# Four semaphores over the whole sequence of gathers, in place of one stop of GpSimd for every group

## The chip, the cores and the metric

One Trainium2 chip, one core. The metric is the device time of the kernel in microseconds (us); every time below is in us unless ns is written. TensorE is called PE, VectorE DVE, ScalarE ACT, GpSimd POOL and SyncE SP, as the profile does.

## The reference: what is computed

One layer of graph attention, and behind it a layer of six experts of which each node takes two. Cut to what matters:

```python
# x: (12500, 256); src, dst: (200000,), dst in rising order; dist: (200000, 1, 1); 4 heads of 64
ft = (layernorm(x) @ W).reshape(n, 4, 64)
e = e_src[src] + e_dst[dst];  e = where(e >= 0, e, 0.2 * e)
a = softmax of e over the edges with the same dst, times dist
x = x + segment_sum(ft[src] * a, dst)          # attention, the "main" stage
x = x + top-2-of-6 experts(layernorm(x))       # three matmul layers for each expert
```

`dst` is `12500 * u**2` for uniform `u`, sorted: the first blocks of nodes have very many edges, the last ones few.

## The kernel before

The kernel runs in stages. Early ones normalise `x`, multiply by `W` and store for every node a row of 264 float32 in DRAM (`table`: 256 features and 8 score words), bring the 200000 edges into columns, and write a plan (`plan`, from `sched`). Then comes `main_stage`, which the change touches, and then `experts`.

The edges are cut into `NG = 196` groups of `GE = 1024` edges, which is `GT = 8` tiles of 128. The nodes are cut into 98 blocks of 128. An *item* is one group together with one block in which it has edges; because both are in order there are 293 items: one for each group and one more for each block that begins. Early in the stage a group has hardly over one item, late it has two. An item does all eight tiles of its group, or four, when its block touches one half only. A *pair* is two finished blocks, whose sums are divided, added to `x`, normalised and stored; there are 49.

What each engine does in `main_stage`:

- POOL goes through the groups in order. For each it issues eight indirect DMAs (`gather(g)`, L1001), each of which fetches 128 rows of `table` (1056 bytes each) into the slot `g % RING` of `rows`; `RING = 4`. Before them it waits, from the fifth group on, that the slot is free (`slot_free`, L1007), and from the second on that the whole group before has landed (`gathered`, L1009). This second wait is the stop in question.
- SP waits that a group has landed and that its row of `dst` is spread (`announce`, L967 to L970), and then raises `group_ready`. In a loop over the groups it first waits, by the plan, that the last item of the group four back is multiplied (`weighted`, L988), raises `slot_free` (L989), issues the next spread of `dst` (`m_drow`, L961), and announces the group before.
- ACT makes for each item the one-hot by node (L1245 and L1248) once its group is announced, and between these the exponentials (L1253 and L1256). It works three items ahead with the one-hots: `exp_item(k + 1)`, then `onehot(k + 3)`.
- DVE has per item the sums of the score parts (L1053), the scores (L1060, L1064), the product of rows and weights (L1085, `m_msg`, which raises `weighted`), the one-hot by edge (L1046) and the addition into the sums (L1101). For a pair, `take_sums` (L1110 to L1132) and `normalize` (L1139 to L1148) come between the items.
- PE looks the scores of the nodes up (L1373) and sums the messages (L1387), and does the router of a pair (L1396 to L1411).

So the order of the stage is set by four queues in program order, by the ring of four slots, and by `plan`, which tells SP when a slot is free and the engines when a pair is due. `experts` begins when all of this is done. It has gathers and scatters of its own on POOL (L1584, L1593), which the change leaves as they are.

Of the kernel before, what the change touches and what calls it, by code (L numbers as in the profile page):

```python
# [18 lines left out]
GT = 8  # L19
GE = GT * P  # L20
NG = -(-E // GE)
# [7 lines left out]
NX = 6  # L29
RH = 128  # L30
RING = 4
NCH = NG // RING
CI = 6
NI = NG + NB - 1
# [2 lines left out]
HI = CI // 2  # L37
NSLOT = NCH * CI
NW = NSLOT + 4
# [24 lines left out]
RSQRT_BITS = float(0x5f3759df)  # L64
assert NG % RING == 0 and NQ * HB == NB and NQ % 2 == 0 and NCH * CI >= NI and EW == 2 * GE and NB % 2 == 0


def not_negative(engine, into, word):

    engine.reg_alu(into, word, 0, ALU.max)  # L70
# [288 lines left out]
def edge_tables(nc, edges, K, sched):  # L359
# [3 lines left out]
    with ExitStack() as ctx:  # L363
# [10 lines left out]
        first = sb("first", [P, 4])  # L374
        item_cmp, group_cmp, pair_cmp = sb("icmp", [P, 320]), sb("gcmp", [P, NG]), sb("pcmp", [NPAIR, 2 * NCH])
        tab = sb("tab", [1, PLAN])
        flat = sb("flat", [1, 320])
        flat_g = sb("flat_g", [1, 320])
        rel = sb("rel", [1, NG])
        pairs = sb("pairs", [1, 2 * NCH])  # L380
        tab_i = sb("tab_i", [1, PLAN], I32)
# [35 lines left out]
        def _(pe):  # L417
# [19 lines left out]
            for ps, column in ((psD[0], in_second), (psD[1], in_first)):  # L437
# [8 lines left out]
            pe.wait_ge(asked, 5)  # L446
            nc.tensor.matmul(psB[0:1, 0:2 * NCH], ones[0:NPAIR, :], pair_cmp[:, :],
                             start=True, stop=True).then_inc(summed, 1)

        @block.vector  # L450
        def _(dve):
# [66 lines left out]
            st.did(v.tensor_copy(pcol[0:NPAIR, :], psC[0:NPAIR, 0:1]))  # L518
            st.did(v.tensor_scalar(pair_cmp[:, :], kk[0:NPAIR, 0:2 * NCH], float(HI), float(HI - 1), ALU.mult, ALU.add))
            st.settle()  # L520
# [21 lines left out]
            st.did(v.tensor_scalar(tab[:, DUE + 1:DUE + NIT], pairs[:, 0:NIT - 1], -float(WAITING), 0.0, ALU.add, ALU.max))  # L542
            st.did(v.tensor_copy(tab[:, REL + RING:REL + NG], rel[:, 0:NG - RING]))
            st.settle()
# [346 lines left out]
def main_stage(nc, K, table, x, sched, ydram, w, out):  # L891
# [3 lines left out]
    with ExitStack() as ctx:  # L895
        def sb(n, s, d=F32):
            return ctx.enter_context(nc.sbuf_tensor("m_" + n, s, d))

        def sem(n):
            return ctx.enter_context(nc.semaphore("m_" + n))  # L900


        rows = sb("rows", [P, RING, GT, LINE])
        drow = sb("drow", [P, RING, GE], U16)
        by_edge = [sb(f"by_edge{i}", [P, GT, P]) for i in range(3)]
# [28 lines left out]
        wd = [a[:, 320:320 + GT * HEADS].rearrange("p (j h) -> p j h", h=HEADS) for a in psA]  # L934
        in_block = [a[:, 384:384 + GT] for a in psA]

        gathered = [sem(f"gathered{i}") for i in range(RING)]
        spread_row = [sem(f"spread_row{i}") for i in range(RING)]
        gathers_seen = sem("gathers_seen")
        group_ready, edge_onehots, looked_up = sem("group_ready"), sem("edge_onehots"), sem("looked_up")  # L940
# [14 lines left out]
        @block.sync  # L955
        def _(sp):
            sp.dma_start(plan[:, :], sched).then_inc(plan_in, 16)

            def spread(at, i):

                sp.dma_start(drow[:, i, :], K.dst_row[bass.ds(at, GE)].partition_broadcast(P))\  # L961
                  .then_inc(spread_row[i], 16)

            def announce(c, i):

                sp.wait_ge(gathered[i], 16 * GT * (c + 1))
                sp.sem_inc(gathers_seen, 1)  # L967
                sp.wait_ge(spread_row[i], 16 * (c + 1))
                sp.sem_inc(group_ready, 1)  # L969

            for i in range(RING):
                spread(i * GE, i)
            sp.dma_start(r1[:, :, :], rw1.rearrange("(c p) n -> p c n", p=P)).then_inc(weights_in, 16)
            sp.dma_start(r2[:, :], rw2).then_inc(weights_in, 16)
            sp.dma_start(rb[:, :], rb1.rearrange("(p a) -> p a", a=1)).then_inc(weights_in, 16)
            for i in range(RING - 1):
                announce(0, i)
            sp.wait_ge(plan_in, 16)
            regs = [sp.alloc_register(f"sp_rel{i}") for i in range(RING)]
            until = [sp.alloc_register(f"sp_until{i}") for i in range(RING)]  # L980
            with sp.Fori(1, NCH) as c:
                sp.load(regs, plan[0:1, bass.ds(c * RING + REL, RING)])
                for r, word in zip(until, regs):
                    not_negative(sp, r, word)
                rel = [sp.snap(r, min_val=1, max_val=NI + 1) for r in until]
                for i in range(RING):
                    at = sp.snap((c * RING + i) * GE)
                    sp.wait_ge(weighted, rel[i])  # L988
                    sp.sem_inc(slot_free, 1)  # L989
                    spread(at, i)  # L990
                    if i:
                        announce(c, i - 1)
                    else:
                        announce(c - 1, RING - 1)
            announce(NCH - 1, RING - 1)

        @block.gpsimd
        def _(pool):
            def gather(g):
                for j in range(GT):  # L1000
                    nc.gpsimd.indirect_dma_start(  # L1001
                        rows[:, g % RING, j, :], None, table,
                        bass.IndirectOffsetOnAxis(ap=K.src_col[:, g, j:j + 1], axis=0)).then_inc(gathered[g % RING], 16)

            for g in range(NG):
                if g >= RING:
                    pool.wait_ge(slot_free, g - RING + 1)  # L1007
                if g:
                    pool.wait_ge(gathered[(g - 1) % RING], 16 * GT * ((g - 1) // RING + 1))  # L1009
                gather(g)  # L1010
            for i in range(RING):
                pool.wait_ge(gathered[i], 16 * GT * NCH)

        @block.vector
        def _(dve):
# [892 lines left out]
def gnn_ffn_kernel(nc, x, src, dst, dist, W, att_src, att_dst, *rest):  # L1908
# [9 lines left out]
    with ExitStack() as ctx:  # L1918
        sb = lambda n, s, d=F32: ctx.enter_context(nc.sbuf_tensor(n, s, d))
        K.ident, K.row = sb("ident", [P, P]), sb("row", [P, P])  # L1920
        K.nid, K.base = sb("nid", [P, NBD]), sb("base", [P, NBD])
        K.far_apart, K.unsorted = sb("far_apart", [1, 1], I32), sb("unsorted", [1, 1], I32)
        K.look = sb("look", [P, NBD, 2 * HEADS])
        K.src_col = sb("src_col", [P, NG, GT], I32)
        K.lg = sb("lg", [P, NB, NX])
        K.dst_col, K.dist_col = sb("dst_col", [P, NG, GT]), sb("dist_col", [P, NG, GT])
        with ExitStack() as early:
            sb = lambda n, s, d=F32: early.enter_context(nc.sbuf_tensor(n, s, d))
            K.every_second = sb("every_second", [P, NPAIR])
            K.wcat = sb("wcat", [P, 2, D + 3 * HEADS])  # L1930
            K.scores = sb("scores", [P, NBD, 2 * HEADS])
            K.rows = sb("rows", [ER, 3, EW])
            constants(nc, K, W, att_src, att_dst)
            features(nc, x, K, table, src, dst, dist, edges)
            sort_edges(nc, K, edges, sorted_edges)
            edge_tables(nc, edges, K, sched)
            lookup_table(nc, K)
        exact_bounds(nc, K, table, sched)
        main_stage(nc, K, table, x, sched, ydram, w, out)
        experts(nc, K, ydram, w, out)  # L1940
# [22 lines left out]
```

## Time and profile before

| | |
|---|---|
| runs without profile, median of 3 | 3641.94 (3638.27 to 3663.85) |
| profiled execution, its own time | 3680.23 |
| its span on the core | 3678.5 |
| POOL busy in the span | 2102.3 (57%), of which gathers (L1001) 1507.0 |
| DVE busy | 1944.0 (53%) |
| PE busy | 2334.5 (63%) |
| ACT busy | 1505.3 (41%) |
| first and last gather of the main stage start at | 242.5 and 2793.7 |

The profiled execution is one run, 38 us (1.05%) above the median of the others. Shares of busy time are averages over the stages; those of the main stage are in the rows further down.

### The profile page before, as it was taken

How to read it: one execution, taken by the hardware profiler on the slowest of the kernel's cores; microseconds unless marked ns; L12 is line 12 of the kernel's file. 1: busy time of each engine (PE TensorE's matmuls, PEld its weight loads, DVE VectorE, ACT ScalarE, POOL GpSimd, SP SyncE). 2: the span in 40 equal slices, each digit the busy share in tenths (PEclk: the TensorE clock that was granted, in tenths of full speed). 3: DMA queues.
4: the chain of work that ended last, by engine and by line, in shares of the span. 5: the costliest groups of instructions: out<-in, count | busy, mean ns of one | idle time of the engine just before them, and what ended most of it. 6: DMA issues, size and time to landing. Idle time of an engine off the chain costs nothing. (4 is left out here: it accounts for less than half of the span.)

```text
span 3678.5 us, 53462 instructions
## 1 busy us (share of the span) xinstructions
PE 2334.5 (63%) x10832; PEld 1847.1 (50%) x10833; DVE 1944.0 (53%) x4409; ACT 1505.3 (41%) x2731; POOL 2102.3 (57%) x2068
## 2 busy tenths in 40 slices
PE   5734455555555555555665656656656689999995
PEld 4523333434434444444544545444445578777774
DVE  5443343444555556556666666666666843333332
ACT  5612222233334334344444445444445345444442
POOL 0026666666666666666656555555541467777775
PEclk9856776777777777777777878777777799999998
DMA  5423444444444444444444444444432424545453
GB/s 163 158 74 108 108 108 105 116 115 109 118 115 123 117 124 115 125 124 127 121 130 122 130 116 123 121 113 115 118 108 61 70 57 79 81 78 82 80 81 50
DMA packets 231558, 394.55 MB, mean 107 GB/s; under 512 B 55832, under 2 KB 148796, under 8 KB 230881
## 3 DMA queue, kind: packets, MB, share of 16 engines
q0 software_dynamic: 114816, 265.53, 30.8%
q1 hardware_dynamic: 76728, 89.16, 9.0%
q10 hardware_dynamic: 39924, 38.86, 3.2%
q8 instruction: 33, 0.54, 0.1%
q14 instruction: 57, 0.47, 0.0%
HBM read 325.36 MB, written 69.42 MB: 107 GB/s over the span
## 5 line engine op out<-in xcount | busy, mean ns | idle before, releaser
L1001 POOL DMA_INDIRECT m_rows<-table,src_col x1568 | 1507.0, 961 | 1085.9 <-issue 480.8
L1387 PE MATMUL m_A<-m_msg,m_by_edge 128*128 128x260 f32 x3920 | 1297.7, 500 | 516.1 <-issue 391.6
L1387 PEld LDWEIGHTS m_A<-m_msg,m_by_edge 128*128 128x128 f32 x3920 | 976.8, 256 | 751.5 <-issue 537.0
L1245 ACT ACTIVATE m_apart<-m_drow,nid 128x1024 bf16 x297 | 341.1, 1148 | 949.0 <-SPq L969 887.2
L1085 DVE TENSOR_TENSOR m_msg<-m_rows,m_A 128x2048 f32<-128x2048 f32 (+1 forms) x294 | 568.2, 1933 | 104.0 <-issue 85.8
L1053 DVE TENSOR_REDUCE m_e_sum<-m_E 128x64 f32<-128x192 f32 x295 | 105.0, 356 | 649.4 <-PE m_E L1373 317.1
L1373 PE MATMUL m_E<-m_look_parts,m_by_node 128*128 x2368 | 109.3, 177 | 519.9 <-ACT m_by_node L1248 494.7
L1373 PEld LDWEIGHTS m_E<-m_look_parts,m_by_node 128*128 128x128 bf16 x2368 | 97.9, 100 | 602.6 <-issue 577.2
L1593 POOL DMA_INDIRECT out<-x_con,x_to_i x206 | 329.4, 1599 | 107.1 <-issue 70.1
L1248 ACT ACTIVATE m_by_node<-m_apart,m_one 128x1024 bf16<-128x1024 bf16 x297 | 341.1, 1149 | 9.7
L1046 DVE TENSOR_TENSOR m_by_edge<-m_A,row 128x1024 f32<-128x1024 f32 (+1 forms) x295 | 307.3, 1042 | 30.6 <-issue 25.1
L1253 ACT ACTIVATE m_z<-m_z 128x32 f32<-128x32 f32 x295 | 67.4, 228 | 490.9 <-DVE m_z L1064 315.7
L1760 DVE TENSOR_TENSOR x_con<-x_X,x_b 128x512 f32<-128x512 f32 x103 | 71.3, 692 | 366.3 <-DMA out<-x_con,x_to_i 329.5
L1584 POOL DMA_INDIRECT x_yr<-ydram,x_from_i x206 | 205.5, 998 | 66.0 <-issue 62.5
L1874 PE MATMUL x_H<-x_yT,x_c 128*128 128x256 f32 x824 | 201.5, 388 | 38.8 <-issue 38.7
L1819 ACT ACTIVATE x_h<-x_H,x_b 128x256 f32<-128x256 f32 x206 | 86.5, 471 | 297.5 <-PE x_H L1874 286.7
L1885 PE MATMUL x_X<-x_c,x_h 128*128 128x256 f32 x824 | 197.4, 383 | 6.6 <-ACT x_h L1819 3.8
L1874 PE MATMUL x_G<-x_h,x_c 128*128 128x256 f32 x824 | 194.7, 379 | 1.3 <-issue 1.3
L1809 ACT ACTIVATE x_c<-x_w 128x512 f32 x309 | 182.8, 627 | 6.0 <-DVEq L1741 5.1
L1874 PEld LDWEIGHTS x_H<-x_yT,x_c 128*128 128x128 f32 x824 | 149.1, 191 | 70.6 <-issue 54.1
L1885 PEld LDWEIGHTS x_X<-x_c,x_h 128*128 128x128 f32 x824 | 157.9, 192 | 29.1 <-issue 7.3
L1874 PEld LDWEIGHTS x_G<-x_h,x_c 128*128 128x128 f32 x824 | 156.5, 190 | 22.9 <-issue 1.6
(249 smaller groups left out, 2400.7 us busy)
## 6 DMA issues: line engine op xcount, KB each, us to landing
m_drow<-dst_row SPq DMA_DIRECT2D x196, 256.0 KB
m_rows<-table,src_col POOLq DMA_INDIRECT x1568
table<-f_rowbuf SPq DMA_DIRECT2D x14, 924.0 KB, 4.9
ydram<-m_y ACTq DMA_DIRECT2D x49, 264.0 KB
m_xb<-in_x ACTq DMA_DIRECT2D x48, 256.0 KB
out<-m_x ACTq DMA_DIRECT2D x48, 256.0 KB
f_xin<-in_x SPq DMA_DIRECT2D x13, 896.0 KB, 6.9
x_w<-in_L_ffn_expert_w SPq DMA_DIRECT2D x18, 256.0 KB, 6.0
```

Source lines behind the costliest of these rows:

```text
L1001: nc.gpsimd.indirect_dma_start(rows[:, g % RING, j, :], None, table, bass.IndirectOffsetOnAxis(ap=K.src_col[:, g, j:j + 1], axis=0)).then_ ...
L1046: v.tensor_tensor(by_edge[q][:, tiles, :], in_block[q][:, tiles].unsqueeze(2).broadcast_to([P, n, P]), K.row[:, :].unsqueeze(1).broadcast_ ...
L1085: v.tensor_tensor(msg[i][:, tiles, 0:D].rearrange("p j (h n) -> p j h n", h=HEADS), rws[:, tiles, 0:D].rearrange("p j (h n) -> p j h n", h ...
L1245: a.activation(apart[i][:, :], drow[:, bass.ds(g % RING, 1), :].rearrange("p a n -> p (a n)"), ACT.Abs, bias=K.nid[:, bass.ds(b, 1)], scal ...
L1248: a.activation(by_node[i][:, :], apart[i][:, :], ACT.Relu, bias=one[:, 0:1], scale=-1.0)\
L1373: m = t.matmul(psE[i][:, 24 * j:24 * j + 24], by_node[i][:, j * P:(j + 1) * P], look_parts[:, bass.ds(b, 1), :].rearrange("p a n -> p (a n)"),
L1387: m = t.matmul(psA[i][:, 0:ROW], by_edge[i][:, j, :], msg[i][:, j, :], start=(j == tiles[0]), stop=(j == tiles[-1]))
L1584: g.indirect_dma_start(yr[t % YR][:, i, :], None, ydram, bass.IndirectOffsetOnAxis(ap=from_i[:, 2 * t + i:2 * t + i + 1], axis=0))\
L1593: g.indirect_dma_start(out, bass.IndirectOffsetOnAxis(ap=to_i[:, 2 * t + i:2 * t + i + 1], axis=0), con[t % CR][:, i, :], None, bounds_che ...
L1809: a.activation(into[t % 2][:, :, :].rearrange("p c n -> p (c n)"), of[:, bass.ds(expert(t), 1), :, :].rearrange("p e c n -> p (e c n)"), A ...
L1874: i = t_.matmul(ps[t % 2][:, m * TILE:(m + 1) * TILE], weight[t % 2][:, c, m * P:(m + 1) * P], of[t % 2][:, c, :], start=(c == 0), stop=(c ...
L1885: m = t_.matmul(psX[t % 2][:, i * D:(i + 1) * D], h2[t % 2][:, c, i * P:(i + 1) * P], c3[t % 2][:, c, :], start=(c == 0), stop=(c == 1))
```

## The change

`gathered`, four semaphores of which each counts the gathers of one ring slot, gives way to `landed`, four semaphores (`LANES = 4`) of which each counts every fourth gather of the whole sequence. The n-th gather waits that gather n - 4 has landed. The wait for the whole group before is taken out. SP's `announce` waits for the four lanes in place of the one slot. The wait for a free slot stays, as do the number of the gathers, their size and their order.

```diff
+LANES = 4
...
-        gathered = [sem(f"gathered{i}") for i in range(RING)]
+        landed = [sem(f"landed{k}") for k in range(LANES)]
...
             def announce(c, i):
 
-                sp.wait_ge(gathered[i], 16 * GT * (c + 1))
+                for k in range(LANES):
+                    sp.wait_ge(landed[k], 16 * (GT // LANES) * (c * RING + i + 1))
                 sp.sem_inc(gathers_seen, 1)
...
             def gather(g):
                 for j in range(GT):
+                    n = g * GT + j
+                    if n >= LANES:
+                        pool.wait_ge(landed[n % LANES], 16 * (n // LANES))
                     nc.gpsimd.indirect_dma_start(
                         rows[:, g % RING, j, :], None, table,
-                        bass.IndirectOffsetOnAxis(ap=K.src_col[:, g, j:j + 1], axis=0)).then_inc(gathered[g % RING], 16)
+                        bass.IndirectOffsetOnAxis(ap=K.src_col[:, g, j:j + 1], axis=0)).then_inc(landed[n % LANES], 16)
 
             for g in range(NG):
                 if g >= RING:
                     pool.wait_ge(slot_free, g - RING + 1)
-                if g:
-                    pool.wait_ge(gathered[(g - 1) % RING], 16 * GT * ((g - 1) // RING + 1))
                 gather(g)
-            for i in range(RING):
-                pool.wait_ge(gathered[i], 16 * GT * NCH)
+            for k in range(LANES):
+                pool.wait_ge(landed[k], 16 * GT * NG // LANES)
```

## Rows read from the trace of the kernel before

**Rows 1.** The page's costliest groups, the gathers: busy, mean ns, idle before.
```profile
L1001 POOL DMA_INDIRECT m_rows<-table,src_col x1568 | 1507.0, 961 | 1085.9 <-issue 480.8
```
**Rows 2.** Windows, gathers alone (L1001): window, length, busy (xcount), PEclk, DMA share, GB/s.
```profile
250.00:750.00 500.00, 306.94 (x322) 0.70 0.40 108
750.00:1250.00 500.00, 306.20 (x320) 0.74 0.43 117
1250.00:1750.00 500.00, 305.98 (x319) 0.77 0.45 123
1750.00:2250.00 500.00, 297.01 (x308) 0.77 0.45 123
```
**Rows 3.** The same windows, DVE's product of each item (L1085).
```profile
250.00:750.00 500.00, 92.90 (x42) 0.70 0.40 108
750.00:1250.00 500.00, 106.19 (x52) 0.74 0.43 117
1250.00:1750.00 500.00, 113.66 (x59) 0.77 0.45 123
1750.00:2250.00 500.00, 119.93 (x65) 0.77 0.45 123
2250.00:2750.00 500.00, 114.37 (x64) 0.76 0.41 116
```
**Rows 4.** The same windows, first instruction of each pair on DVE (L1110).
```profile
250.00:750.00 500.00, 0.17 (x1) 0.70 0.40 108
750.00:1250.00 500.00, 1.03 (x6) 0.74 0.43 117
1250.00:1750.00 500.00, 1.82 (x10) 0.77 0.45 123
1750.00:2250.00 500.00, 2.47 (x13) 0.77 0.45 123
2250.00:2750.00 500.00, 2.63 (x15) 0.76 0.41 116
```
**Rows 5.** Timeline of POOL: start, length, instruction [idle before <- what ended it].
```profile
279.23 0.95 POOL L1001 DMA_INDIRECT m_rows<-table,src_col  x1 [2.17 <-DMA m_rows<-table,src_col]
280.49 0.96 POOL L1001 DMA_INDIRECT m_rows<-table,src_col  x1 [0.30 <-issue]
...
291.62 0.95 POOL L1001 DMA_INDIRECT m_rows<-table,src_col  x1 [2.62 <-SPq L989]
```
**Rows 6.** POOL's waits, 250 to 2250: us in total, times, longest us.
```profile
POOL m_rows L1001 <- SPq L989: 218.8, 82, 4.8
POOL m_rows L1001 <- DMA m_rows<-table,src_col: 205.8, 76, 4.1
```
**Rows 7.** ACT's waits in the same stretch, same columns.
```profile
ACT m_apart L1245 <- SPq L969: 887.2, 119, 22.8
```
**Rows 8.** POOL's waits, 2250 to 2800.
```profile
POOL m_rows L1001 <- SPq L989: 129.6, 21, 10.5
...
POOL m_rows L1001 <- DMA m_rows<-table,src_col: 50.9, 16, 4.4
```
**Rows 9.** Timeline of DVE where it is the later one: items and one pair.
```profile
2402.61 1.22 DVE L1085 TENSOR_TENSOR m_msg<-m_rows,m_A 128x1024 f32<-128x1024 f32 x1 [0.32 <-issue]
...
2405.59 0.17 DVE L1110 TENSOR_SCALAR m_den<-m_sums 128x8 f32 x1
...
2410.46 2.29 DVE L1085 TENSOR_TENSOR m_msg<-m_rows,m_A 128x2048 f32<-128x2048 f32 x1
...
2416.49 1.22 DVE L1085 TENSOR_TENSOR m_msg<-m_rows,m_A 128x1024 f32<-128x1024 f32 x1 [0.30 <-issue]
...
2419.30 0.17 DVE L1139 TENSOR_TENSOR m_newton<-m_inv 128x2 f32<-128x2 f32 x1
...
2423.66 2.29 DVE L1085 TENSOR_TENSOR m_msg<-m_rows,m_A 128x2048 f32<-128x2048 f32 x1
```
**Rows 10.** Timeline of POOL in the experts: a scatter behind a wait.
```profile
3002.39 1.62 POOL L1593 DMA_INDIRECT out<-x_con,x_to_i  x1 [0.46 <-issue]
```
**Rows 11.** Windows, all engines, the stretch of a burst with the largest DMA share.
```profile
1020.00:1028.00 8.00, 5.62 (x16) 4.29 (x16) 4.45 (x10) 1.77 (x4) 5.97 (x7) 0.75 0.60 167
```

## The prediction

> **What bounds the kernel now.** The page comes first: the costliest group of the main stage is the gathers, 1568 of 961 ns, and POOL stands idle before them for another 1085.9 us, of which only 480.8 is the plain step from one to the next [rows 1]. The chain that ended last doesn't help, since followed back it stays within the experts. So I read the main stage in windows of 500 us, first the gathers [rows 2], then the items [rows 3] and pairs [rows 4] that the other engines got done. What to see there: up to 1750 the gathers come at the same even rate (322, 320 and 319 in 500 us, so 12.4 to 12.5 us for a group of eight), while the work behind them rises from 42 items and 1 pair to 59 items and 10 pairs. A rate that doesn't follow the load belongs to the feeder. From about 2000 on it is the other way: gathers fall off (308 in the fourth window), items stay at 65 and 64. The waits say the same. Up to 2250 ACT waits 887.2 us in 119 pieces for a group to be announced [rows 7]; there the consumers (ACT, DVE and PE together) starve. After 2250 POOL waits up to 10.5 us for a slot [rows 8]; there they are the bound.
>
> The timeline shows what POOL's 12.5 us are [rows 5]: an issue of 0.95 to 0.96, a step of 0.30, so 1.26 per gather and 10.1 for eight, and once a group a stop. The stop is 2.17 in the third group, where the landing is the only thing waited for, and 2.62 later, where the instruction has two waits. The row of 2.62 names SP's slot_free, but it is the same stop: SP waits for that same landing in its own queue before it raises slot_free, and the two come together. 158 such stops (82 + 76) up to 2250 make 424.6 us, 2.69 each [rows 6].
>
> **What the change removes.** The stop. In its place stays the plain step of 0.30, so a group loses 2.6 - 0.3 = 2.3 us and POOL's floor is 12.5 - 2.3 = 10.2 us (which also keeps the rare longer steps inside the 12.5). It removes no gather and no byte.
>
> **What it adds on POOL: a wait before each gather.** Whether it blocks: a waiting gather starts 2.17 us after the end of the issue it waits for [rows 5]. Gather n waits for n - 4, whose issue ended three gathers and four steps earlier: 3 x 0.96 + 4 x 0.30 = 4.08 us. There are 1.9 us to spare, so the lane wait has always been met. The longest stop found was 4.4 us [rows 8], with the double wait's 0.45 inside it (2.62 - 2.17), so 3.95: even that is inside 4.08. Cost nothing. Were the landing later, gathers would be slowed one by one; that is a rival below.
>
> What a met wait costs by itself no row shows. From below: nothing, since it can be settled while the gather before still runs, and it adds nothing to the 0.96. From above: the scatter in the experts, which has two waits and follows directly upon other work, started 0.46 after the end of the one before, 0.16 over a plain step [rows 10], and part of that is a real wait. Two waits for 0.16 are 0.08 for one, 0.64 per group. I take 0, as the row is itself an upper bound, and keep 0.64 per group for the range.
>
> The Trainium skill (Perfetto Trace Analysis, section DMA Instruction, SWDGE (GPSIMD)) has the sequencer push such an instruction into a wait queue and go on to decode the next, so that a wait that is met there is hidden. By it the sum stays with 0; no row here tells it from 0.08.
>
> The first gather of a group has two waits, slot and lane. Its lane wait is for the fifth gather of the group before and has the same 1.9 us to spare; the double wait's 0.45 still fits under that.
>
> **What it adds on SP: four waits for one.** SP has nothing else to do between two groups. Queued behind them are the spread of dst, the next slot_free and the announcement for which ACT waits. They pass one after the other once the last gather has landed, some 0.1 us each at most (my estimate: below the 0.30 step of POOL), which delays one announcement and not the distance between two. slot_free for group g comes after the announcement of group g - 2, which has landed over one whole group (10 us) before POOL asks. Cost nothing; if SP's cover were gone it would be 0.3 us a group.
>
> **What is late next.** Either the ring or the consumers. Ring: the slot for group g is free once the last item of g - 4 is multiplied. ACT's order (one-hot of k + 3 after the exponential of k + 1) makes that wait for g - 3 to be announced at most, which is two groups less a landing before POOL wants the slot: 2 x 10.2 - 2.2 = 18 us. Behind the announcement stand one or two steps of 5 to 9 us [rows 9]. So the ring has some 9 us to spare with one item to a group, and takes up a pair.
>
> Consumers: their own rate is seen from 2250 to 2750, where 500 us hold 64 items and 15 pairs [rows 3, 4]. Two prices follow from this, with one equation. The ends of L1085 are 2403.83, 2412.75, 2417.71 and 2425.95 [rows 9]: 8.92 with the first half of a pair between, 4.96 with none, 8.24 with the second half. So a pair costs at least 3.96 + 3.28 = 7.2, and an item then at most (500 - 15 x 7.2) / 64 = 6.12. Or an item costs the least, 4.96, and a pair (500 - 64 x 4.96) / 15 = 12.2. With these, the work of each earlier window, against POOL's 10.2 for each of its groups [rows 2 to 4]:
>
> 250 to 750: 42 items, 1 pair: 264 by the first pair of prices, 221 by the second; POOL 40.25 x 10.2 = 411. Saved 89.
> 750 to 1250: 52, 6: 361 or 331; POOL 408. Saved 92.
> 1250 to 1750: 59, 10: 433 or 415; POOL 407. Saved 67 or 85.
> 1750 to 2250: 65, 13: 492 or 481; POOL 393. Saved 8 or 19.
> After 2250 nothing, as the consumers are the bound there already.
>
> The sums are 256 and 285. I take the first and subtract 15: near the crossing (10 pairs of the third window and about half of those beside it) the work comes in clumps, and I put one us for each of some 15 pairs; early items are also more often of eight tiles than late ones, which speaks for the lower sum too. So 241.
>
> **The sum.** On the profiled execution 3680 - 241 = 3439. It lies 38 us above the median of the runs; nothing tells where these 38 are, so the same 241 is taken off the median: 3642 - 241, rounded 3402. Of the stage's stops (424.6) a little over half comes back, because the consumers take over at about 1400.
>
> **The rivals.**
>
> *The consumers are slower in the earlier part than late prices say.* Each item would cost more with eight tiles on PE and DVE, or the ring would bind around pairs. At 7 us an item and 7.2 a pair the third window would be 485 and nothing would come back there, the second stays at 408. Saved 89 + 92 = 181, less the 15: 3476. For it: full items are the majority early. Against: in rows 9 the intervals before full products (4.96 to 8.9) are not longer than before half ones. A tenth.
>
> *A met wait isn't free.* With 0.64 a group, over the 120 groups of the first three windows, 77 us come off where POOL is the bound, but in the third window the consumers cover most of it. So 50 to 77: 3452 to 3479. It would need 0.29 a gather to undo the whole change. A tenth.
>
> *Landings get later and the lanes throttle: slower.* Without the stop POOL never lets the DMA queues run empty. If a landing took x from the end of its issue to the start of the waiting gather, a lane of four would give 2 x (0.96 + x) per group. This beats today's 12.5 up to x = 5.3, against 2.17 now. At x = 6 a group costs 13.9, 1.4 more over 160 groups to 2000: 3642 + 225 = 3867; 5.6 would be 3741. For it: stops grow to 4.4 late in the stage, where other DMAs are about [rows 8]. Against: the DMA engines are busy 0.40 to 0.45 on average [rows 2] and 0.60 in a burst beside a spread of dst [rows 11], and a fifth more traffic fits in. 0.06.
>
> *DVE holds GpSimd up.* If issues become longer the closer DVE's work stands, a fifth more overlap would lengthen them. From the first to the fourth window the mean issue rises from 306.94 / 322 = 0.953 to 297.01 / 308 = 0.964, while items go from 42 to 65 [rows 2, 3]. Even 0.1 more per gather, ten times that, would be 0.8 a group over 100 groups: 3482. The Trainium skill (SBUF: State Buffer, section Who interferes with whom) speaks of an exclusive lock: DVE copies in a two-port mode keep GpSimd from writing descriptors. The trace agrees with no such thing at this size. 0.03.
>
> *The change doesn't do what it says.* If POOL waited at every gather until the one before was settled, or if SP's slot_free were the true end of the stops, the 2.6 would stay and the time within 1%, 3606 to 3678. Rows 5 speak against it: the stop is there in the third group, which has no slot to wait for. 0.05.
>
> **How the numbers follow.** Forecast 3402, its own range 3370 (the sum of 285 less 15) to 3450: 0.64. Slower consumers 0.10, the price of waits 0.10, both faster by over 1%. No change 0.05; DVE 0.03, faster; landings 0.06, slower; more than forecast, below 3370, 0.02. 1% (36 us) is about what a measurement of this kernel can tell from no change. Faster 0.89, same 0.05, slower 0.06. For 8 in 10 the range runs from 3370 to 3480, where the two rivals end.
>
> **What the profile after would show.** Gathers of the first windows 1.26 us apart without a gap at the head of a group, so 390 instead of 322 in 500 us. No wait of POOL for a DMA. POOL's waits for slot_free beginning at about 1150 to 1200 (where 1400 of before then lies) and growing. ACT's wait for announcements falling from 887 to about 450. The end of the main stage near 2600, the experts as long as before. Wrong would be: steps of 0.35 or more between gathers, stops at every gather, issues longer than 1.0, or a slot wait already in the first 500 us.

## Result: the change made the kernel 9% slower where the prediction's trace was taken, and 11% faster in another session

| | us | ratio to before [95%] |
|---|---|---|
| before, median of 4 | 3648.48 (3638.27 to 3663.85) | |
| after, median of 4 | 3979.93 (3976.66 to 3983.42) | 1.0905 [1.086, 1.0949] |
| after, profiled execution | 3983.42, span 3981.7 | |
| forecast | 3402 (3370 to 3480) | 0.93 |

The kernels ran in sessions of two kinds, told apart by what the kernel before takes in them (medians): 3646 to 3685, called condition X here, or 3565 to 3567, condition Y. The prediction's trace and this result are from X. The same change measured in Y gives 3172.84, ratio 0.8895 [0.8881, 0.891]. Ratios are only taken between runs of one session. The granted clock doesn't tell the two apart: for the kernel before it is 0.79 to 0.81 in X and 0.80 to 0.81 in Y. Two single executions, one of e6 below (3734.89, granted clock 0.61) and one of e8 (4175.94, clock 1.0), lie far from the other three of their kernels (clock 0.81 to 0.83) and are left out of the medians given here.

The page of after (line, engine, operation, count; busy time and mean of one in ns; idle before and what ended most of it) has the gathers at the old duration, [rows 1] read 961, with still more idle time before them:

```profile
L1006 POOL DMA_INDIRECT m_rows<-table,src_col x1568 | 1505.2, 960 | 1394.5 <-SPq L991 898.4
```

The idle time is put down to SP's `slot_free`. POOL's waits over the whole run (total us, count, longest), against [rows 6]:

```profile
POOL m_rows L1006 <- SPq L991: 898.4, 115, 15.5
POOL m_rows L1006 <- DMA m_rows<-table,src_col: 7.0, 18, 1.0
```

The lanes hardly ever stop POOL: 7.0 us in 18 pieces of 1568. It stands 898.4 us for slots. The windows of the gathers (us of the window; busy and count; granted clock, DMA share, GB/s), against [rows 2]:

```profile
250.00:750.00 500.00, 299.76 (x315) 0.67 0.39 105
750.00:1250.00 500.00, 280.18 (x292) 0.70 0.39 106
1250.00:1750.00 500.00, 263.72 (x275) 0.72 0.38 103
1750.00:2250.00 500.00, 241.89 (x254) 0.72 0.36 101
```

and those of the items (L1088, L1085 before), against [rows 3]:

```profile
250.00:750.00 500.00, 88.32 (x40) 0.67 0.39 105
750.00:1250.00 500.00, 94.59 (x46) 0.70 0.39 106
1250.00:1750.00 500.00, 97.33 (x50) 0.72 0.38 103
1750.00:2250.00 500.00, 97.64 (x52) 0.72 0.36 101
```

None of the gathers' rates is POOL's floor, which would be 500 / 1.26 = 397. The consumers do 40, 46, 50, 52 items where they did 42, 52, 59, 65. In the first window they had starved before, and now they do fewer and still hold POOL up. The DMA share is the same or lower, so the transfers aren't the load. The timeline shows what happens. POOL first (start, duration, idle before and what ended it):

```profile
624.87 0.96 POOL L1006 DMA_INDIRECT m_rows<-table,src_col  x1 [0.30 <-issue]
626.13 0.95 POOL L1006 DMA_INDIRECT m_rows<-table,src_col  x1 [0.31 <-issue]
635.02 0.95 POOL L1006 DMA_INDIRECT m_rows<-table,src_col  x1 [7.94 <-SPq L991]
```

and PE over the same stretch:

```profile
614.30 4.52 PE L1390 MATMUL m_A<-m_msg,m_by_edge 128*128 128x260 f32 x10 [2.28 <-DVE m_msg L1088]
620.42 0.38 PE L1390 MATMUL m_A<-m_msg,m_by_edge 128*128 128x260 f32 x1 [1.60 <-issue]
623.21 0.59 PE L1390 MATMUL m_A<-m_msg,m_by_edge 128*128 128x260 f32 x1 [2.41 <-issue]
626.00 0.59 PE L1390 MATMUL m_A<-m_msg,m_by_edge 128*128 128x260 f32 x1 [2.20 <-issue]
628.10 0.59 PE L1390 MATMUL m_A<-m_msg,m_by_edge 128*128 128x260 f32 x1 [1.51 <-issue]
```

POOL issues every 1.26 us, undisturbed. The ten matmuls that start at 614.30 take 4.52 together, and then they come singly, 2.1 to 2.8 us apart, each after a wait for "issue", that is for nothing the profile shows. These four begin within 0.03 us of a register or arithmetic instruction of ACT that takes 0.69 to 0.70 us (620.39, 623.19, 625.98 and 628.09). I read this as slow dispatch and no dependency. The sequencers' own small instructions (here SP's register operations, L962; shortest/median/longest in ns) show it too. After, in X, and under it before:

```profile
L962 SPq FUSED_REGOPS  x192: 42/46/701, 286.0 to 3091.2; - x192
```

```profile
L961 SPq FUSED_REGOPS  x192: 42/46/248, 280.8 to 2784.7; - x192
```

Half of them take 46 ns, but some 0.70 us. Counted over SP, ACT and DVE between the first and the last gather (register, move, arithmetic and branch instructions, in the trace FUSED_REGOPS, MOVE, ALU_OP and COMPARE_BRANCH, of 0.6 to 0.8 us), after has 949 of 11578, before 363 of 11479. Where they crowd they begin together on several engines (616.87 on all three), and the next mostly begin 0.70 or 1.40 us later. I call such a time a slow stretch. It comes late in a row of gathers without a stop (no idle time of 0.45 us or more between them). In after, 2% of these instructions are slow while the first to third gather of a row goes out, 8% at the fourth to seventh, 37% at the eighth to eleventh, 40% at the twelfth to fifteenth, 55% at the sixteenth to 21st, and 71% beyond.

The waits of PE and DVE between 250 and 2250 grow with them ("remote" is an end that the profile can't name). After, and under it before:

```profile
PE m_A L1390 <- issue: 496.2, 172, 14.6
DVE m_e_sum L1056 <- remote: 480.2, 51, 19.2
```

```profile
PE m_A L1387 <- issue: 249.6, 126, 8.5
DVE m_e_sum L1053 <- remote: 97.3, 27, 6.2
```

The total of PE's row is no measure of the stretches by itself: the same row of the change in Y, where there are none, is not much below that of before. Besides, the traces of X have lost part of the semaphore updates (table further down), so a wait can stand under these two names because its end is missing.

```profile
PE m_A L1390 <- issue: 211.7, 143, 5.2
```

What shows that the stretches were already in the kernel before is the count of slow instructions, 363. No gather has more than seven ahead of it without a stop there, and at the eighth 31% are slow.

### The profile page after: what moved, and what is told of

Its sections match the earlier page's. It is cut to its first block and busy times, and to the rows that moved or that the text cites. A ratio compares the mean times of both kernels' runs of the same rounds, so it can differ in the third digit from the quotient of the medians.

```text
span 3981.7 us, 53754 instructions
## 1 busy us (share of the span) xinstructions
PE 2348.7 (59%) x10832; PEld 1854.0 (47%) x10833; DVE 1935.9 (49%) x4409; ACT 1508.8 (38%) x2731; POOL 2099.5 (53%) x2068
## 5 line engine op out<-in xcount | busy, mean ns | idle before, releaser
L1006 POOL DMA_INDIRECT m_rows<-table,src_col x1568 | 1505.2, 960 | 1394.5 <-SPq L991 898.4
L1390 PE MATMUL m_A<-m_msg,m_by_edge 128*128 128x260 f32 x3920 | 1315.8, 500 | 1021.3 <-issue 704.8
L1088 DVE TENSOR_TENSOR m_msg<-m_rows,m_A 128x2048 f32<-128x2048 f32 (+1 forms) x294 | 568.2, 1933 | 145.1 <-issue 126.6
L1251 ACT ACTIVATE m_by_node<-m_apart,m_one 128x1024 bf16<-128x1024 bf16 x297 | 341.0, 1148 | 11.6 <-issue 1.4
L1376 PE MATMUL m_E<-m_look_parts,m_by_node 128*128 x2368 | 117.4, 176 | 212.6 <-issue 164.7
L1376 PEld LDWEIGHTS m_E<-m_look_parts,m_by_node 128*128 128x128 bf16 x2368 | 111.0, 100 | 275.8 <-issue 239.5
```

The costliest lines, as they stand in the source:

```text
L1006: nc.gpsimd.indirect_dma_start(rows[:, g % RING, j, :], None, table, bass.IndirectOffsetOnAxis(ap=K.src_col[:, g, j:j + 1], axis=0)).then_ ...
L1088: v.tensor_tensor(msg[i][:, tiles, 0:D].rearrange("p j (h n) -> p j h n", h=HEADS), rws[:, tiles, 0:D].rearrange("p j (h n) -> p j h n", h ...
L1251: a.activation(by_node[i][:, :], apart[i][:, :], ACT.Relu, bias=one[:, 0:1], scale=-1.0)\
L1376: m = t.matmul(psE[i][:, 24 * j:24 * j + 24], by_node[i][:, j * P:(j + 1) * P], look_parts[:, bass.ds(b, 1), :].rearrange("p a n -> p (a n)"),
L1390: m = t.matmul(psA[i][:, 0:ROW], by_edge[i][:, j, :], msg[i][:, j, :], start=(j == tiles[0]), stop=(j == tiles[-1]))
```

## The experiments

### First series: which part of the change (condition X, before 3650.28)

Two theories stood against each other. A: the missing stop slows the other engines. B: the waits that the change adds (lanes on POOL, four on SP) cost; the texts on record of this series call SP's share C, and from the third series on C is another theory, that it depends on where and when the kernels run.

**e1**, the change with the stop put back, as a wait for the last gather of the group before:

```diff
             for g in range(NG):
                 if g >= RING:
                     pool.wait_ge(slot_free, g - RING + 1)
+                if g:
+                    pool.wait_ge(landed[LANES - 1], 16 * (GT // LANES) * g)
                 gather(g)
```

> The changed kernel with the stop back: at the head of each group POOL waits for the last gather of the group before. Theory A (the missing stop: while gathers follow each other without a pause, the instructions that each engine's own sequencer does, registers, branches, waits, take 0.70 us in place of 0.03 to 0.08, and everything behind the gathers slows) expects the time of before, 3640 to 3680. Theory B (a wait in front of every gather is what disturbs) and theory C (SP's four waits for one make the slots late) expect it to stay near 3980.

Measured 3645.37, 0.9991 [0.9979, 1.0003]. Lanes and SP's four waits together cost nothing; B is refuted.

**e2**, the kernel before without its stop, and no lanes:

```diff
-                if g:
-                    pool.wait_ge(gathered[(g - 1) % RING], 16 * GT * ((g - 1) // RING + 1))
```

> The kernel before with the stop alone taken out: no lanes, no wait per gather, SP waits for one semaphore. Theory A expects it as slow as the changed kernel, 3950 to 4000. Theories B and C expect what I had forecast for the change, near 3400.

Measured 3971.87, 1.0883 [1.0865, 1.0901]. The missing stop alone makes the whole loss. SP's register operations (L961) read as in after, even longer:

```profile
L961 SPq FUSED_REGOPS  x192: 42/46/1408, 282.0 to 3061.5; - x192
```

**e3**, the change with `LANES = 2`, so that each gather waits for the last but one, and gathers come 1.71 us apart on average:

```diff
-LANES = 4
+LANES = 2
```

> The changed kernel with two lanes in place of four: a gather waits for the last but one, which lands 2.17 us after its issue ended, so gathers come every (0.96 + 2.17) / 2 = 1.57 us, 12.5 us per group as before, but evenly and without a stop. Theory A in its strict form (a pause is needed) expects about 3950 or more. A second form, A2 (what counts is how many gathers come per us; a backlog fills at 1.26 us each and drains at 1.57), expects 3600 to 3700. B expects 3980 or more.

Measured 3790.43, 1.0376 [1.0356, 1.0396]. Its gathers (timeline of POOL):

```profile
601.65 0.95 POOL L1006 DMA_INDIRECT m_rows<-table,src_col  x1 [0.79 <-DMA m_rows<-table,src_col]
602.91 0.95 POOL L1006 DMA_INDIRECT m_rows<-table,src_col  x1 [0.30 <-DMA m_rows<-table,src_col]
604.68 0.95 POOL L1006 DMA_INDIRECT m_rows<-table,src_col  x1 [0.82 <-DMA m_rows<-table,src_col]
606.45 0.95 POOL L1006 DMA_INDIRECT m_rows<-table,src_col  x1 [0.82 <-DMA m_rows<-table,src_col]
...
620.03 0.95 POOL L1006 DMA_INDIRECT m_rows<-table,src_col  x1 [1.30 <-DMA m_rows<-table,src_col]
623.23 0.95 POOL L1006 DMA_INDIRECT m_rows<-table,src_col  x1 [2.25 <-issue]
```

13.67 us for a group is more than before (13.02 in the profiled execution) and more than the 12.5 expected, and the time follows. But only 10 of 11682 sequencer instructions are slow, against 363 before. The gathers don't come evenly, as the expectation had it. Of the 1567 steps between them 594 are below 1.4 us, 552 are 1.6 to 1.9, and 334 are longer than that, where the kernel before has 210 such steps; two steps below 1.4 never follow each other. So the slow instructions go when no more than two gathers follow each other closely. Whether the mean pace does it or the many short pauses, this run can't tell.

**e4**, the kernel before with its stop in front of every second group only:

```diff
-                if g:
+                if g % 2:
```

> The kernel before with the stop in front of every second group only, so 16 gathers in a row. Theory A expects a time between the two kernels, 3700 to 3950, as the slow stretches begin after some 5 gathers in a row and would now cover half or more of each 22 us. B and C expect about half the gain I had forecast, 3520.

Measured 3887.28, 1.0658 [1.0635, 1.068]. Sixteen gathers in a row bring 6.6 of the 8.8% that e2 loses: three quarters, a dose between eight in a row and no stop at all.

### Second series: what it is in the gathers (turned out to be condition Y, before 3567.28)

All four of this series came out below everything that was expected of them. The diffs leave out the lines that declare `pad`, `padded` and `blank`.

**e5**, the change with gathers of 256 bytes a row out of `x` instead of 1056 out of `table`; the other three quarters of the messages and the scores are left out:

```diff
-                        rows[:, g % RING, j, :], None, table,
+                        rows[:, g % RING, j, 0:64], None, x.rearrange("n (a d) -> (n a) d", a=4),
...
+            nc.gpsimd.memset(rows[:, :, :, :], 1.0).then_inc(blank, 1)
+            pool.wait_ge(blank, 1)
```

> The changed kernel, but each gather fetches 256 bytes a row in place of 1056, from x in place of the table; three quarters of the bytes and the scores are left out (the rest of each row stays a constant), so the output isn't the reference's. Number, order and pace of the gathers, of the landings and of the waits are the same. Theory A-bytes (the slow stretches come from the traffic: packets and bytes of the gathers fill something that drains in the stop) expects them gone or nearly, and 3350 to 3500. Theory A-issue (they come from POOL's issuing itself or from the landings' semaphore counts, of which there are as many as before) expects 3900 to 4000.

Measured 3172.68, 0.8894 [0.8879, 0.8908], no slow instruction at all.

**e6**, the kernel before with the stop replaced by work on POOL, a memset of 2400 columns ahead of each group:

```diff
-                if g:
-                    pool.wait_ge(gathered[(g - 1) % RING], 16 * GT * ((g - 1) // RING + 1))
+                if g:
+                    pool.wait_ge(padded, g - 1)
+                    nc.gpsimd.memset(pad[:, :], 0.0).then_inc(padded, 1)
```

> The kernel before with the stop replaced by a memset of 2400 columns on POOL, about 2.1 us by the 1.8 us that one of 2048 columns takes, plus a step: POOL pauses the issuing for as long as the stop did, but waits for no landing. Theory A2 (the pace counts) expects the time of before within 1.5%, 3600 to 3700. A theory that the landing itself must be awaited, or that POOL must stand idle, expects 3900 to 4000.

Measured 3493.39 (median of three), 0.9791 [0.9772, 0.9811]. In Y this says only that a group with the memset takes POOL 12.1 us; whether waiting for the landing matters for the slow stretches stays untested, as there are none in Y.

**e7**, the change with a memset of one column ahead of every gather:

```diff
+                    if n:
+                        pool.wait_ge(padded, n)
+                    nc.gpsimd.memset(pad[:, :], 0.0).then_inc(padded, 1)
```

> The changed kernel with a memset of one column on POOL ahead of each gather, so that gathers come about 1.4 us apart (1.26 plus 0.1 and some step), evenly, 11.2 us a group. A2 with a threshold below 1.4 expects no slow stretches and a time under that of before, 3450 to 3550. With the threshold between 1.4 and 1.57 it expects slow stretches and 3700 to 3900.

Measured 3175.47, 0.8902 [0.8887, 0.8917]. The memset goes into the 0.30 step, and gathers stay 1.26 apart (timeline of POOL, from the later f3):

```profile
600.08 0.11 POOL L1008 MEMSET m_pad<- 128x1 f32 x1
600.38 0.96 POOL L1011 DMA_INDIRECT m_rows<-table,src_col  x1 [0.19 <-issue]
601.64 0.96 POOL L1011 DMA_INDIRECT m_rows<-table,src_col  x1 [0.19 <-issue]
```

So e7 has the pace of the change, and yet was 11% faster than before. Either the memset between gathers heals (D), or something of the session had changed (C); before itself was 2.3% faster than in the first series. e5's time couldn't be read as an effect of bytes until this was settled.

**e8**, the same with 256 columns, which brings the gathers to 1.45 apart (the texts on record say 1.51 from the fourth series on):

> The same with 256 columns, gathers about 1.6 to 1.7 us apart, 13 us a group. A2 expects no slow stretches, POOL as the bound to the end of the stage (196 x 13 = 2550 us of it, as long as the stage of before), so 3600 to 3700; without slow stretches the consumers keep up to the end, as they did with two lanes at 13.6 to 13.9 us a group.

Measured 3399.40 (median of three), 0.9532 [0.9513, 0.9551].

### Third series: the change again beside the memsets (condition X, before 3646.6)

**f1** is the change, **f2** the kernel before, **f3** is e7, **f4** has e7's memset once a group (`if g:` ahead of `gather(g)`) instead of once a gather.

> The changed kernel itself, unedited, beside the next three on one chip. The last four runs were on another chip than the first ones (the kernel before took 3567 there, 3650 here), and none of their traces held a slow stretch. Theory C (the slow stretches come with the chip) expects that on a chip where the kernel before takes 3567 the change takes 3150 to 3250 as well, and where that takes 3650 it takes 3980. Theory A expects about 1.09 of the kernel before on either chip.

> The kernel before, unedited, for its trace on this chip. C expects no slow stretches where it takes 3567 and some where it takes 3650. A expects the late part of each burst of eight to have them on both.

> The changed kernel with the memset of one column ahead of each gather, again. Gathers stayed 1.26 us apart with it, so the pace is not what it changed. Theory D (another POOL instruction between two gathers by itself ends the slow stretches) expects 0.89 of the kernel before on every chip. C expects the same time as f1 within 1.5%: about 3180 on a chip of 3567, about 3980 on one of 3650.

> The changed kernel with one memset of one column at the head of each group, eight gathers in a row. D with a backlog that one other instruction clears expects no slow stretches and 0.89; D strictly (between any two gathers) expects most of the slow stretches, 1.05 or more; C expects the time of f1.

Measured: f1 3971.82, 1.0895 [1.0862, 1.0927]; f2 3646.0, 1.0002 [0.9988, 1.0017]; f3 3982.66, 1.0934 [1.0906, 1.0962]; f4 3979.6, 1.0917 [1.0892, 1.0942]. The memset heals nothing: e7's kernel, letter for letter, is at 0.89 in one session and at 1.09 in the other. D is refuted.

### Fourth series: all of it once more (condition Y, before 3567.12)

**g1** is e5, **g2** is e6, **g3** is e8 and **g4** the change itself.

> As e5_narrow_rows: 256 bytes a row from x in place of 1056 from the table; three quarters of the bytes and the scores are left out. Where the kernel before takes 3650: if bytes fill what makes the stretches, below 3400; if issuing or the landings' counts do, 3900 or more. Where it takes 3567, 3173 as before, which tells nothing.

> As e6_busy_stop: the kernel before with a memset of about 2 us for the stop. Where the kernel before takes 3650: within 1.5% of it if only the pace counts, 3900 or more if POOL has to wait for a landing. Where it takes 3567: 3496.

> As e8_pad_256: the changed kernel with a memset of 256 columns ahead of each gather, gathers evenly 1.51 us apart, 12.1 us a group. Where the kernel before takes 3650: if 1.51 is slow enough for the stretches not to form (at 1.70 they didn't, with two lanes), 3400 to 3450, faster than before; if what counts is the mean pace and 1.51 is above what drains, 3600 to 3900. Where it takes 3567: 3399.

> The changed kernel, unedited. Where the kernel before takes 3650: 1.09 of it, 3980, as twice before. Where it takes 3567: 3160 to 3190, 0.89 of it, since the one-column memset changed nothing in the other condition; theory D (the memset mattered there) expects 3800 or more.

Measured: g1 3173.62, 0.8897 [0.8882, 0.8912]; g2 3492.82, 0.9793 [0.9777, 0.9809]; g3 3402.43, 0.9534 [0.9518, 0.9549]; g4 3172.84, 0.8895 [0.8881, 0.891]. The session decides the sign of the change: 1.0895 in f1, 0.8895 in g4, one kernel. It isn't the position of the chip in the machine: chip 1 was in X in the third series and in Y in the second. In Y narrow rows gain nothing over the change (3173.62 and 3172.84), since bytes bound nothing there. SP's register operations in g4, against the two rows in the section on the result:

```profile
L962 SPq FUSED_REGOPS  x192: 42/46/47, 278.1 to 2289.1; - x192
```

None is over 47 ns. The windows of g4's gathers, items (L1088), and of the pairs in the last window (L1113):

```profile
250.00:750.00 500.00, 378.27 (x397) 0.75 0.50 135
750.00:1250.00 500.00, 379.28 (x395) 0.80 0.53 146
1250.00:1750.00 500.00, 376.09 (x392) 0.84 0.56 155
1750.00:2250.00 500.00, 340.23 (x352) 0.85 0.52 146
```

```profile
250.00:750.00 500.00, 115.93 (x53) 0.75 0.50 135
750.00:1250.00 500.00, 135.34 (x68) 0.80 0.53 146
1250.00:1750.00 500.00, 146.48 (x78) 0.84 0.56 155
1750.00:2250.00 500.00, 145.87 (x81) 0.85 0.52 146
```

```profile
1750.00:2250.00 500.00, 3.28 (x18) 0.85 0.52 146
```

and its waits from 250 to 3100 with the same columns as before:

```profile
POOL m_rows L1006 <- SPq L991: 70.1, 28, 6.1
ACT m_apart L1248 <- SPq L971: 652.4, 134, 19.2
```

That is mostly the forecast's picture: gathers close to the 390 in 500 us that it names, and POOL the bound for three windows. It differs in that the slot waits, 70.1 us in 28 pieces, all but one (0.7 us) come after 1750, where the forecast had them begin at 1150 to 1200, and in that ACT's wait for announcements is 652.4, where it had 450.

### Last two: pace and session crossed

**h1** is e8 (gathers 1.45 apart), **h2** is e3 (two lanes); I hoped for each in the other condition.

> As e8_pad_256, gathers evenly 1.51 us apart. Where the kernel before takes 3650: 3400 to 3450 if no stretches form at 1.51, 3600 to 3900 if they do. Where it takes 3567, 3400 as twice before, and the question stays open.

> As e3_two_lanes. Where the kernel before takes 3567: 3770 to 3800 if the two conditions differ by the slow stretches alone, since this kernel had hardly any in the other; a good deal less, 3650 to 3720, if everything is a few per cent faster there. Where it takes 3650: 3790 again.

Measured: h1 3396.6 beside 3565.22, 0.953 [0.9513, 0.9547], Y for the third time. h2 3791.68 beside 3684.67, 1.0298 [1.0279, 1.0316]: X, and a worse one. Before lost 34 us against the first series, while two lanes took the same 3790 to 3792, with 6 slow instructions of 11678. So X varies in strength, and the two-lane kernel didn't feel it here.

The traces side by side; worked out from the main stage's first and last gather, from the counts of instructions of 0.6 to 0.8 us as above, and from the landing updates of the 1568 gathers that the trace has kept (16 a gather, 25088 were due):

```
                          cond.  stage us       per group    slow instr.      updates kept
before                      X     2551.3         13.02        363 of 11479           7073
f2 (before)                 X     2519.9         12.86        2.9%                   7761
e1 stop and lanes           X     2514.8         12.83        3.2%                   7502
e4 stop every second        X     2756.2         14.06        6.2%                   4797
e2 no stop, no lanes        X     2828.8         14.43        7.4%                   4087
after                       X     2857.7         14.58        949 of 11578           4018
f1 (after)                  X     2845.4         14.52        7.5%                   4042
f3 / f4 small memsets       X     2856.4/2858.4  14.57/14.58  7.8% / 8.4%     3476 / 3953
e3 / h2 two lanes           X     2680.0/2674.8  13.67/13.65  10 and 6 of 11680  17836 / 16697
e5 / g1 narrow rows         Y     2053.9/2052.0  10.48/10.47  0             24916 / 25004
e7 memset of 1 column       Y     2060.0         10.51        0                     24745
g4 (after)                  Y     2054.8         10.48        0                     24911
e8 / g3 / h1 1.45 apart     Y     2284.4/2289.7/2284.2  11.65 to 11.68  0    24999 / 25005 / 25025
e6 / g2 busy stop           Y     2383.3/2372.9  12.16/12.11  0             25012 / 25029
```

What the span holds beside this stage is 1110 to 1129 us in all twenty traces, so what sets the kernels and the conditions apart lies in the main stage. The kernel before has no trace in Y, but its 3567 less such a rest leaves 12.5 us a group, which is the prediction's reading. From there the time is 3567 + 196 x (us per group - 12.5): 3171 for 10.48 (measured 3173), 3402 for 11.66 (3397 to 3402), 3491 for 12.11 (3493), and for two lanes in X 3794 for 13.66 (3792). The same sum holds for the others in X (3975 for the 14.58 of after), so it tells where the time is and not what made a group longer. In Y that is POOL's own pace: eight steps of 1.26 are 10.1 us against the 10.48 measured, eight of 1.45 are 11.6 against 11.66. In X the kernels with gathers 1.26 apart take longer than in Y at the same pace, by 81 us with rows of eight (3648 for 3567) and by some 800 without a stop (3972 to 3983 for 3173).

## Why the prediction was wrong

**The step that failed** is "Consumers: their own rate is seen from 2250 to 2750, where 500 us hold 64 items and 15 pairs". It carries the rate of the other engines from one stretch to denser gathers as if it were a property of theirs, and no rival had them slow down with POOL's pace. In X they did: by the upper of the item's prices the 40 items of after's first window are 40 x 6.12 = 245 us of 500, and yet POOL waited 103.6 us for slots in it. The gain of 241 turned into a loss of 331. That the missing stop made this difference is shown by e1, e2 and e4. That it goes by way of the slow instructions is what the traces suggest: their share rises with the loss from e1 to e4 to e2, and the same kernel in Y has neither.

The rate was wrong for Y as well, the other way. In g4 the fourth window holds 81 items and 18 pairs, which by those prices would have been 81 x 6.12 + 18 x 7.2 = 625 us in 500. The prices were mis-sized. The "least" item, 4.96, is the distance to a half product, and both longer distances of [rows 9] end in full ones, so part of what was put down to the pair is the item's size. For the same reason those rows don't bear out the prediction's remark that the distances before full products are not longer than before half ones. Without a pair between, the shortest distance between the ends of two products is 3.6 for a half and 5.0 for a full product, in g4 as in the trace of before, and the window that the rate was read from had slow stretches in it too (107 of its 2676 small instructions). So most of the stage is POOL's in Y, and the change saves (12.5 - 10.48) x 196 = 396 of the 2.3 x 196 = 451 that the stops cost, where the forecast counted on 241: measured 394 (3567.12 - 3172.84), below the forecast's own low end.

**POOL's floor, 10.2 a group**: right; in g4 a group takes 10.1 to 10.25 on average up to group 150, 1.26 between gathers in both conditions.

**A met lane wait costs nothing**: right. e1 has 1564 of them and is at 0.9991; the steps of after stay 0.30. The Trainium skill (Perfetto Trace Analysis, section DMA Instruction, SWDGE (GPSIMD)) has such an instruction pushed into a wait queue while the sequencer goes on to the next; the trace agrees with a met wait that is hidden there: 0.30 before, 0.30 after. The landings stayed inside the 4.08 us of cover in all but 18 cases, 7.0 us together, so the rival of late landings didn't occur.

**SP's four waits cost nothing**: right, by e1.

**The sum** 3642 - 241 is 3401, not 3402, which changes nothing.

**The other rivals**: DVE doesn't hold GpSimd up, with issues of 960 ns against 961. That the change does nothing, because slot_free is the true end of the stops, is refuted by e2 and g4.

**The sign on record** that would show it wrong, "a slot wait already in the first 500 us", is there: between 250 and 750 POOL waits for SP's slot 103.6 us in 14 pieces.

```profile
POOL m_rows L1006 <- SPq L991: 103.6, 14, 11.7
```

**What the rows of before could have told.** 363 of the 11479 register, move and branch instructions of SP, ACT and DVE in the stage take 0.6 to 0.8 us where half of them take 0.05 or less, and even among SP's at L961 some take 248 ns where the median is 46. I read the engines' waits and never the length of these instructions. PE's 249.6 us of waits for nothing shown would not have told: in Y, without a slow instruction, they are 211.7. Also the 38 us between the profiled execution and the median, of which the prediction says that nothing tells where they are, fit X: there single runs of the kernel before go from 3635.39 to 3686.12, in Y from 3564.27 to 3572.59.

**What stays open.** What the sequencers share that clogs. Two candidates are only argued. One is the recording of events: the traces of X lack 29 to 86% of the gathers' landing updates, those of Y at most 1.4%, and the kernels with the most slow instructions lack the most, roughly. That is not merely what slow engines leave behind: two lanes lack 29 and 33% with 10 and 6 slow instructions, and in the experts, where X has no slow instruction either, its traces keep 4685 to 4952 of the DMAs' updates and those of Y 7244 to 7246. But it doesn't show that the recording slows anything: both may come from a third thing, the rate of records alone isn't it (the change leaves the same 53754 instructions in 3167.9 us in Y as in 3981.7 in X), and each timed run reports a clock and a span, so it isn't known here whether any of them ran without recording. The Trainium skill (NOTIFIC — the notification-queue block, section 7.1) has the block's internal pipeline always hold its producers back rather than lose a record, which would make engines slow when it fills; its section 10 has the emission of a record cost the engine zero cycles and no overflow at 6.6 million records a second. No run here shows the block itself. The other candidate is whatever brings the sequencers their instructions: PE, SP, ACT and DVE slow together, while POOL, with few and long instructions, does not. No run touched that, and the trace speaks against plain instruction fetches: the DMA queues of kind "instruction" carry 18 packets in the main stage of after, and 18 in that of g4. The gathers' own packets aren't slower in X either, 167 ns on average in after and 170 in g4. Whether the gathers' bytes or the number of their issues and updates is what fills it couldn't be told either: the narrow rows met Y both times, as did the pace of 1.45 all three times. Two lanes weren't run in Y. What in a session makes X or Y isn't known, nor whether it can change between two executions.

**Which version to take.** In Y the change as it is (3172.84) is the fastest that computes the whole result; the memset of one column (3175.47) equals it. In X nothing run was faster than before; e1 equals it. Gathers 1.45 apart gain 4.7% in Y and might be free of slow stretches in X, as two lanes were, but that wasn't measured.

## What to carry to other kernels

A wait that looks like waste on the feeding engine may be a pause that the other engines need, whatever it is that recovers in it (not shown here): before taking it away, look at the longest of their smallest instructions beside the median. Waits that end with no named cause are a weaker sign, since they are there without slow stretches as well. A consumer's rate read from one stretch holds only at that stretch's density of feeding. Run a change with much finer-grained traffic in more than one session, with the kernel before beside it each time; here that decided the sign.

## What the runs showed of the hardware

- While indirect gathers of 128 rows x 1056 bytes go out 1.26 us apart, register, move and branch instructions of the sequencers of SP, ACT and DVE can take 0.70 us in place of a median of 0.05, in some sessions, and PE then gets one matmul per 2.1 to 2.8 us. POOL's own issues (0.96) don't change. In after such instructions are 2% up to the third gather in a row, 8% up to the seventh, 37% at the eighth to eleventh and 71% from the 22nd on. They are almost absent with two lanes (10 of 11682), where no more than two gathers follow each other closely, and wholly absent in other sessions at 1.26 (0 of 11594 in g4).
- A memset of one column between two gathers costs no time on POOL: it lies in the step of 0.30, and 1.26 stays. With 256 columns (0.34 us) the gathers are 1.45 apart.
- With each gather waiting for the last but one, many start 0.82 us after the end of the issue before them, others 0.30 or up to 3.7 us; the mean is 1.71 us from gather to gather in place of 1.26.
